# Attention-like filter and routed experts on one core: a deeper fold in the fourth group, and a new order at the seam between filters and experts

## The reference, cut to what matters

```python
# 16 sequences x (128 channels x 256 positions), fp32
x = x + tanh(g_xattn[0]) * filtered(ctx, ctx, layernorm(x), ssm_kernel, D)   # head_dim 8, 16 heads
x = x + tanh(g_ffn[0])   * moe(layernorm(x))

# filtered(k, v, q): kv = k x v inside each head, filtered along the positions, times q
kv  = einsum('bhil,bhjl->bijhl', k_, v_)
y   = irfft(rfft(kv, 2L) * rfft(ssm_kernel, 2L))[..., :L]
out = einsum('bijhl,bhil->bjhl', y + kv * D, q_)

# moe(xt): 2048 tokens of 256 elements, 8 experts, hidden 352, room for 256 tokens each
probs = softmax(xt @ Wg);  eidx = argmax(probs);  gate = probs[eidx]
pos   = place of the token among its expert's;  keep = pos < 256
xd[eidx * 256 + pos] = xt            (kept tokens only)
h     = silu(xd @ W1) * (xd @ W3);   out = (h @ W2)[slot of the token] * gate * keep
shared = silu(xt @ sw1) * (xt @ sw3) @ sw2
return out + shared
```

## Time and profile before

| what | value |
|---|---|
| median of 3 runs | 214.21 us (214.07 to 214.26) |
| profiled execution, device time | 214.29 us |
| its span | 212.6 us |
| PE busy | 198.7 us, 93% of the span |
| DVE busy | 159.9 us, 75% |
| POOL busy | 123.8 us, 58% |
| ACT busy | 91.9 us, 43% |

### The profile page before, as it was taken

One profiled execution on the slowest core, in us unless ns is written; L12 is line 12 of the kernel. 1 busy time (PEld: TensorE's weight loads), 2 busy tenths in 40 slices (PEclk: granted clock), 3 DMA queues, 4 the chain that ended last, 5 costly groups with the idle time before them and its releaser, 6 DMA issues.

```text
span 212.6 us, 4239 instructions
## 1 busy us (share of the span) xinstructions
PE 198.7 (93%) x1441; PEld 184.0 (87%) x1441; DVE 159.9 (75%) x518; ACT 91.9 (43%) x182; POOL 123.8 (58%) x129
## 2 busy tenths in 40 slices
PE   5979999899999999999999998999999999999960
PEld 5957789679998989988989998999999999999950
DVE  4798788966998987589867877776856995878530
ACT  2242733193443651322348258654373445624400
POOL 4379999274648599614583253370072687677671
PEclk9999999999999999999999999999999999999996
DMA  5799993000000010010201799845537689422221
GB/s 158 245 339 359 371 396 133 0 0 3 5 0 0 0 53 17 33 54 0 92 10 50 229 357 360 298 125 138 166 106 245 187 261 329 128 78 72 67 91 49
DMA packets 21497, 29.77 MB, mean 140 GB/s; under 512 B 2834, under 2 KB 18970, under 8 KB 21476
## 3 DMA queue, kind: packets, MB, share of 16 engines
q1 hardware_dynamic: 18964, 23.24, 33.3%
q0 software_dynamic: 2304, 6.05, 8.7%
q10 hardware_dynamic: 208, 0.22, 0.4%
HBM read 21.32 MB, written 8.45 MB: 140 GB/s over the span
## 4 chain that ended last, share of the span: by engine, by line
PE 83%; DVE 4%; DMA 4%; issue 3%; ACT 2%; POOLq 1%; ACTq 0%; SPq 0%; DVEq 0%; POOL 0%
PE fb L1294 16%; PE z L1294 14%; PE z L1206 11%; PE tp L1231 10%; PE z L1203 6%; PE z L1315 6%; PE z L1329 5%; PE fb L1329 4%; DMA x_sb<-x 3%; PE fb L1315 2%; DVE terms L509 2%; PE tp L1243 2%; PE tp L1340 2%; DMA dcol<-skip_d 1%; DVE stats L923 1%
## 5 line engine op out<-in xcount | busy, mean ns | idle before, releaser
L509 DVE TENSOR_TENSOR terms<-z,qr 128x512 f32<-128x512 f32 (+2 forms) x192 | 48.9, 326 | 6.5 <-PE z L1206 6.4
L1206 PE MATMUL z<-kv,toep 128*128 128x288 f32 x128 | 41.5, 406 | 0.0
L1294 PE MATMUL fb<-xTh,wh_gu 128*128 128x256 f32 (+1 forms) x104 | 31.9, 306 | 0.2 <-issue 0.2
L490 POOL TENSOR_TENSOR kv<-ct 128x768 f32<-128x768 f32 x15 | 27.4, 1827 | 6.6 <-PE z L1206 3.3
L1203 PEld LDWEIGHTS z<-kv,toep 128*128 128x128 f32 x128 | 22.1, 190 | 9.2 <-issue 4.8
L716 POOL DMA_INDIRECT kv<-out,tok x16 | 20.4, 1273 | 16.3 <-DMA out<-x_sb 11.7
L1203 PE MATMUL z<-kv,toep 128*128 128x144 f32 x128 | 26.8, 291 | 2.8 <-DVE terms L509 1.9
L1294 PE MATMUL fb<-xTl,wh_gu 128*128 128x256 f32 (+1 forms) x104 | 29.0, 279 | 0.0
L1294 PE MATMUL fb<-xTh,wl_gu 128*128 128x256 f32 (+1 forms) x104 | 29.0, 279 | 0.0
L662 POOL TENSOR_TENSOR terms<-terms 128x512 f32<-128x512 f32 x16 | 20.2, 1281 | 14.1 <-DVE terms L509 14.0
L667 POOL DMA_INDIRECT xd_scratch<-xrow,dest x16 | 16.7, 1044 | 17.1 <-DVE xrow L1002 7.3
(11 more groups left out here) (154 smaller groups left out, 417.9 us busy)
## 6 DMA issues: line engine op xcount, KB each, us to landing
terms<-w SPq DMA_DIRECT2D x16, 352.0 KB, 4.3
ct<-ctxt SPq DMA_DIRECT2D x3, 768.0 KB, 8.8
xd_scratch<-xrow SPq DMA_DIRECT2D x4, 516.0 KB, 9.7
kv<-xd_scratch SPq DMA_DIRECT2D x8, 258.0 KB, 3.4
out<-x_sb SPq DMA_DIRECT2D x8, 256.0 KB, 2.6
terms<-w SPq DMA_DIRECT2D x8, 256.0 KB, 4.7
x_sb<-x SPq DMA_DIRECT2D x3, 512.0 KB, 6.0
toep<-kskip_scratch SPq DMA_DIRECT2D x3, 512.0 KB, 9.8
```

The lines of the kernel that those rows point to most:

```text
L490: eng.tensor_tensor(dst, left, right, ALU.mult)
L509: return eng.tensor_tensor(view(terms, t0 + row * TROW + col, [[64, 2], *td]), view(src, zo, [[512, 2], *zd]), view(qr, q0 + qo, [[CW, 2], ...
L1206: mm = pe.matmul(z[s % 2][:, k, 0:KVH], toep[:, h, 0:P], view(kv, o, [[1, KVH]]), start=False, stop=True, skip_group_check=True)
L1294: mm = pe.matmul(bank[0:rows(blk, c), m * 256:(m + 1) * 256], wt[w % 2][:, col:col + rows(blk, c)], xt[:, place, k, first:first + 256], st ...
```

## The change

The fourth group's 8 rows are folded to 2: POOL adds a second, half as large addition behind the first, with a wait on its own semaphore between them, and `terms_of(3)` is 2, so PE does 8 transposes a half. Slot 29 holds no shared use any more; the uses behind it move by one slot, except for the router's chunks, and ("gu", 4, 0) goes behind the router's chunks of the fourth group. The third group's logits fall due two slots later, behind the fourth group's norm; its exp, places, gates and scatters follow at 12 and 13. The fourth group's logits, exp, gates, places and scatters fall due one slot later. The second group's scatters, two of which stood in slot 28 and two in slot 32, are all in slot 32.

```diff
+FILTER_ONLY = 29
-THIRD_STEPS = {"ln2_apply": 4, "logits": 9, "exp": 9, "places": 10, "gate": 10, "scatter": 10}
-OWN_STEPS = (FIRST_STEPS, {}, THIRD_STEPS)
+THIRD_STEPS = {"ln2_apply": 4, "logits": 11, "exp": 12, "places": 13, "gate": 13, "scatter": 13}
+SECOND_STEPS = {"scatter": 16}
+OWN_STEPS = (FIRST_STEPS, SECOND_STEPS, THIRD_STEPS)
 LAST_STEPS = {
     "turn_r0": 1, "turn_r1": 1, "residual0": 2, "residual1": 2, "ln2_stats": 2, "ln2_scale": 2, "ln2_apply": 2,
-    "turn_xT": 4, "tokens_low": 5, "logits": 7, "exp": 7, "gate": 8, "places": 9, "scatter": 9,
+    "turn_xT": 4, "tokens_low": 5, "logits": 8, "exp": 8, "gate": 9, "places": 10, "scatter": 10,
 }
-SCATTER_REST = {24: 0, CONV: 1}
+SCATTER_REST = {24: 0}
...
-    return TERMS if g < FULL_TERMS else TERMS // 2
+    return TERMS if g < FULL_TERMS else TERMS // 4 if g == NG - 1 else TERMS // 2
...
-    rest += [("gu", 4, 0), ("y", 3, 0), ("gu", 6, 2), ("gu", 7, 2), ("gu", 4, 1), ("gu", 5, 0), ("gu", 5, 1), ("y", 4, 0),
+    rest += [("y", 3, 0), ("gu", 6, 2), ("gu", 7, 2), ("gu", 4, 0), ("gu", 4, 1), ("gu", 5, 0), ("gu", 5, 1), ("y", 4, 0),
...
-        elif s >= REST_SLOT:
+        elif s >= REST_SLOT and s != FILTER_ONLY:
...
-                pool.tensor_tensor(low, low, high, ALU.add).then_inc(folded, 1)
+                ins = pool.tensor_tensor(low, low, high, ALU.add)
+                if g == NG - 1:
+                    chain(ins)
+                    low, high = (view(terms, first_head(g, u) * 64 + i * 2 * TROW, [[TROW, 2], [1, 128]])
+                                 for i in range(2))
+                    ins = pool.tensor_tensor(low, low, high, ALU.add)
+                ins.then_inc(folded, 1)
```

## The result

The changed kernel takes 219.79 us (median of six runs, 218.82 to 221.14); the kernel before took 214.21 us. The ratio is 1.027, with a 95% interval of 1.0226 to 1.0310. So the change costs 5.6 us. The direction was as forecast, and the size was not: 216.5 us had been predicted, and the upper end of the range was 219.0. Lines shift by eight: L1239 is the turn, L747 and L945 the two halves of the norm, L675 the scatters, L1323 the post.

What follows compares the result with a forecast made beforehand. TensorE, with 83% of the chain, was taken as the bound; fourth scatter landing at 120.1 plus a 17.7 us chain put the post at 137.8 instead of 135.30, 2.5 us later: 216.5 us, range 213.9 to 219.0.

Steps and rivals of the forecast that it cites:

- Part 1, the fold on TensorE: Fourth group's turn: 16 of 32 transposes gone, 1.9 us less on TensorE; second addition on POOL 0.7 us, hidden.
- Part 2, the use taken out: Slot 29: TensorE meets the last filters 1.4 us sooner; last fold ends at 110.8, turn starts at 111.5.
- Part 3, start of the fourth scatter: Second group's scatters, all behind the last fold: the fourth starts at 115.75, 2.2 us into five experts' loads.
- The start-up share: From the last wait to the first scatter 0.88 us; were it short, the fourth scatter would start 0.7 us sooner.
- its landing: Fourth scatter takes 4.7 us to land, less half the doubtful start-up: landed at 120.1, ends 118.55 and 122.65.
- my first rival: Quick landing: fourth scatter lands after about 2.8 us despite the weights; 214.9 us, chance 0.24.
- Part 4, the chain from landing to post: From the fourth scatter's landing to half group 4's down projection (the post): 17.7 us, post at 137.8.
- The wait of 0.7 us for the logits: TensorE, done with ("gu", 4, 0), waits 0.7 us for the fourth group's router logits, as in the kernel before.
- the load behind the copy: ScalarE loads the silu's table, 1.28 us, only behind its waiting copy of the router's logits.
- ahead of the fourth tokens: Sign in the changed profile: TensorE waits before the fourth group's tokens, as the norm starts only at about 120.
- PE itself is no hindrance: Ahead of ("gu", 6, 2), the first router use: TensorE stands at the fourth tokens by 119 to 120.
- The rival of the deep queue: All five expert loads slow the fourth scatter to a 6.9 us landing: post at 140.35, 219.2 us, chance 0.14.

Runs made afterwards that it cites:

- the warmed one: Changed kernel plus 26 unused identity transposes on TensorE ahead of its wait for the fourth norm: 218.67 us, ratio 1.0177.
- weights held: Changed kernel, but SyncE begins the experts' weights only when the second group's four scatters have landed: 215.35 us, ratio 1.0031.
- the fold alone: Kernel before with only the deeper fold of the last group, all orders as before: 215.17 us, ratio 1.0019.
- changed, weights held, early silu: Changed kernel with weights held until the four scatters land, plus a one-column silu behind the third group's exponential: 214.01 us, ratio 0.9997.

## Why the prediction was wrong in size

The mechanism came as predicted, and two terms of the sum failed: the landing was sized too small, and the clock behind TensorE's idle time was left out. Point by point, in the profiled execution, where the post is at 142.21 and had been put at 137.8, 4.4 us too early:

- **Part 1, the fold on TensorE: right.** 1.96 us for 16 transposes. The second addition takes 0.74 us where 0.7 was taken.
- **Part 2, the use taken out: right in its steps.** The last fold ends at 111.7, the turn starts at 112.49 where 111.5 was said; 0.64 us of that is the shift that this execution has at the mark already. The fold is hidden.
- **Part 3, start of the fourth scatter: right.** 116.52 against 115.75, 0.64 of the 0.77 from the same shift. The start-up share that I had called doubtful is there, 0.79 us ahead of the first scatter.
- **Part 3, its landing: a term mis-sized.** 5.9 us in the changed kernel and 6.0 in the warmed one. I had taken 4.7 from the nearest row, less 0.35 for the doubt. That is 1.6 us of the miss. The row of 4.7 was met by one expert's weights and then a fetch of tokens; here SyncE went on issuing weights, and 6.9 was the nearer end. Distance from the first issue was the wrong measure of likeness: the second scatter, which started 0.5 us before that issue, took 4.4 us, and the third, 0.8 us behind it, took the full 5.9. What was issued while a scatter was under way counted too. From the rule of the Trainium skill that a DMA engine takes the queues in turn, packet by packet ("DMA: Bandwidth & Descriptors", "Queues, rings and completion order"), I had drawn that the landing might stay near 2.8 us, my first rival. The trace contradicts what I had drawn from it: the scatter behind 2 us of backlog takes twice as long as the quiet one. Whether the engines take turns, no run here shows.
- **Part 4, the chain from landing to post: right.** 17.7 us predicted, 17.54 (weights held) and 17.57 (warmed) measured where the clock was undisturbed. The wait of 0.7 us for the logits and the load behind the copy stand where they were said to be.
- **A term that was missing: the clock.** I had TensorE waiting "ahead of the fourth tokens", said so under what would show it, and went on counting its work at full speed. "PE itself is no hindrance" ahead of the first router use held at full clock (with the weights held the low halves are ready at 124.01 and the use starts at 124.11) and failed at half clock (128.40 and 130.63). From norm to post it is 19.69 instead of 17.57: 2.1 us in this execution.

The sum is 0.8 + 1.6 + 2.1 = 4.5 us, for 4.4 observed, as the chain was 0.1 us shorter than predicted. Counted from the mark, without the shift of 0.64 us, the post is 6.3 us late instead of 2.5. In the medians the miss is 3.3 us (219.79 against 216.5): the profiled execution is 1.35 us above its median, and the shorter ones lose less to the clock.

By ratios it closes as well, within the uncertainty given above: the change costs 2.7%; with the weights held 0.3% remain, so landing and clock together are 2.4% or 5.1 us, of which the clock is 1.9 and the landing 3.2 (3.3 from the traces, 5.9 less 2.65). The rival of the deep queue, 219.2 us, came nearest, but by luck: its landing of 6.9 us was 1.0 us too long, and that stood in for part of the clock, which it left out as well. The price of the first rival, 214.9 us for a quick landing, is what holding the weights brings: 1.0031 of 214.21 is also 214.9.

Why is the gain given back even with a quick landing? The start of the fourth norm on ScalarE, counted from the mark, and the way from there to the post, in us:

| kernel | mark to norm | norm to post | mark to post |
|---|---|---|---|
| before | 21.37 | 13.98 | 35.35 |
| the fold alone | 22.10 | 13.89 | 35.99 |
| changed | 21.93 | 19.69 | 41.62 |
| changed, warmed | 21.94 | 17.57 | 39.51 |
| changed, weights held | 18.59 | 17.54 | 36.13 |
| changed, weights held, early silu | 18.72 | 16.49 | 35.21 |

With the fold alone the norm comes no sooner. With the rest of the change and the weights held it comes 2.8 us sooner, but the new order has put 3.6 us more of ScalarE's and VectorE's work between the norm and the post. 1.05 us of that is the silu's table load, and taking it away removes the last 0.3% of the loss; the other 2.5 us are what the prediction had lined up behind the landing, the third group's choice above all, and were not tried one by one. In neither case does TensorE's work ahead of the norm set the time of the post, so 1.9 us less of it buys nothing. That TensorE held 83% of the chain of waits was true of the whole and misleading for this seam; its small waits of 0.63 and 0.21 us fit another chain that runs right beside it.

## What to carry to other kernels

When work before a seam gets shorter on one engine, look at which transfers its end releases: here a turn that came and ended sooner sent the weights out 3.5 us earlier, into a scatter that a norm waited for, and one more wait ahead of the weights took away nearly all the loss. A step that is brought forward wins only if nothing is queued behind it in its place: here the norm could come 2.8 us sooner, and 3.6 us of other work then stood between it and the post. If a forecast has TensorE idle for some microseconds, price the clock behind that idle time too, from a row of the same kernel if there is one. A small wait on the bounding engine is a hint that a second chain runs close behind it, and that a saving on that engine alone may bring little.

## What the hardware did that was not expected

- An idle time of TensorE of 3.35 us brought 6.8 us at the 1.2 GHz level, the first of them while it was still idle, and cost 2.1 us on the path; one of 3.59 us did the same, and two of 2.56 and 2.57 us brought a window of 4 us to 0.57. Idle times of 1.87, 1.33 and 0.94 us in other runs left the clock at 1.00. How much was lost differed between executions of the same kernel (average clock 0.974 to 0.987). The Trainium skill ("TensorE: Matmul & The Clock Gate", "What's actually happening") says that the gate follows how busy the array has been lately; the runs agree, and the warmed one shows that transposes of no use keep it open.
- The same indirect scatter of 128 rows, issued by GpSimd, lands after 2.65 us on quiet engines, after 4.4 us when it starts 0.5 us ahead of a long row of weight loads from SyncE, after 5.9 to 6.0 us when it starts 0.8 or 2 us into it, and after 6.9 us deep in them.
- In the three runs of the changed kernel with the norm moved, a silu on ScalarE began 1.2 us after the matmuls that feed it had ended, with ScalarE idle (at 117.66 in the one shown). No cause was found.
